# A feature-cross network on one core: a fifth PSUM bank for layer 2, products that read SBUF, and a sum split between GpSimd and VectorE

## The reference

```
x0 = e                                   # (512, 39, 16)
z  = einsum('bfd,bgd->bfgd', x0, xk)     # every pair of fields, kept per embedding column d
x1 = einsum('bpd,pm->bmd', z(x0, x0), f0)
x2 = einsum('bpd,pm->bmd', z(x0, x1), f1)
x3 = einsum('bpd,pm->bmd', z(x0, x2), f2)
h  = concat(sum_d x1, sum_d x2, sum_d x3, dense_ctx)
y  = relu(relu(h @ W1 + b1) @ W2 + b2) @ W3
```

## Time and profile before

| | us |
|---|---|
| median of three runs | 735.24 |
| profiled execution | 735.52 |
| its span, first to last instruction | 733.7 |
| TensorE busy in it | 671.3 (91%) |
| VectorE busy | 626.0 (85%) |
| GpSimd busy | 459.2 (63%) |
| ScalarE busy | 390.5 (53%) |

### The profile page before, as it was taken

The page is one execution under the profiler, slowest core; times in us unless marked ns, Lnnn a source line. Parts: engine busy times, 40 slices in busy tenths (PEclk is TensorE's granted clock), DMA queues, the critical chain, the costliest instruction groups (busy, mean ns, idle before and its releaser), DMA issues.

```text
span 733.7 us, 11667 instructions
## 1 busy us (share of the span) xinstructions
PE 671.3 (91%) x3072; PEld 523.1 (71%) x3072; DVE 626.0 (85%) x2018; ACT 390.5 (53%) x1163; POOL 459.2 (63%) x404
## 2 busy tenths in 40 slices
PE   0187989999999999999999999999999999999977
PEld 0165767676767778787867778787867778787856
DVE  3646999999999898999789898999789898999750
ACT  0325565665656565656456565656456565655321
POOL 6345979586868776775658776775658675552220
PEclk9998999999999999999999999999999999999989
DMA  9814640404040313112030312112040303000000
GB/s 145 155 37 123 208 107 8 106 6 105 7 106 7 97 17 78 34 47 66 5 105 7 99 14 77 35 42 70 5 106 5 104 10 88 16 1 0 1 1 0
DMA packets 70261, 41.27 MB, mean 56 GB/s; under 512 B 47298, under 2 KB 55042, under 8 KB 70067
## 3 DMA queue, kind: packets, MB, share of 16 engines
q1 hardware_dynamic: 60438, 36.45, 19.7%
q0 software_dynamic: 5248, 1.29, 2.1%
q10 hardware_dynamic: 4508, 2.80, 2.0%
HBM read 38.55 MB, written 1.94 MB: 55 GB/s over the span
## 4 chain that ended last, share of the span: by engine, by line
PE 67%; DVE 19%; issue 5%; DMA 3%; POOL 2%; ACT 2%; ACTq 1%; SPq 0%; DVEq 0%; POOLq 0%
PE y L779 17%; PE y L781 14%; PE y L780 14%; DVE scaled L682 14%; PE late L797 4%; PE side L786 3%; PE acc L754 3%; PE acc L753 3%; PE acc L759 3%; PE side L743 2%; DMA s_sb<-in_w_dram 2%; PE late L808 2%; DVE z L652 1%; PE late L830 1%; DVE x_parts L658 1%
## 5 line engine op out<-in xcount | busy, mean ns | idle before, releaser
L682 DVE SCALAR_TENSOR_TENSOR scaled<-y,x_rows,scaled 128x128 f32<-128x128 f32 x1728 | 465.4, 342 | 53.5 <-PE y L781 35.6
L526 ACT ACTIVATE scaled<-y,x_rows 128x128 f32<-128x128 f32 x768 | 218.8, 367 | 165.0 <-PE y L781 150.3
L779 PE MATMUL y<-w_hi,x_parts 128*128 128x512 f32 (+1 forms) x640 | 277.7, 434 | 18.2 <-DVE scaled L682 8.8
L781 PE MATMUL y<-w_hi,x_parts 128*128 128x512 f32 (+1 forms) x640 | 249.0, 389 | 0.0
L780 PE MATMUL y<-w_lo,x_parts 128*128 128x512 f32 (+1 forms) x640 | 248.6, 389 | 0.0
L426 POOL TENSOR_TENSOR z_parts<-z,z_parts 117x512 fp32r<-117x512 f32 (+1 forms) x108 | 139.5, 1291 | 88.8 <-ACT z_parts L480 67.1
L779 PEld LDWEIGHTS y<-w_hi,x_parts 128*128 128x128 f32 x640 | 120.8, 189 | 80.8 <-DVE scaled L682 50.6
L415 POOL DMA_INDIRECT emb_quads<-in_small_tables_dram,quad_rows x144 | 138.0, 959 | 32.7 <-issue 15.5
L781 PEld LDWEIGHTS y<-w_hi,x_parts 128*128 128x128 f32 x640 | 120.7, 189 | 24.9
L434 POOL TENSOR_TENSOR sum<-scaled 128x512 f32<-128x512 f32 x64 | 82.8, 1293 | 84.0 <-DVE scaled L682 83.6
L780 PEld LDWEIGHTS y<-w_lo,x_parts 128*128 128x128 f32 x640 | 121.5, 190 | 14.2
(11 more groups left out here) (42 smaller groups left out, 352.0 us busy)
## 6 DMA issues: line engine op xcount, KB each, us to landing
z<-x_turned SPq DMA_DIRECT2D x309, 78.0 KB
x_three<-x_turned SPq DMA_DIRECT2D x48, 78.0 KB
x_turned<-emb_quads SPq DMA_DIRECT2D x160, 8.0 KB
w_sb<-in_w_dram SPq DMA_DIRECT2D x1, 2496.0 KB, 9.6
emb_quads<-in_small_tables_dram,quad_rows POOLq DMA_INDIRECT x144, 2.4
x_turned<-emb_singles SPq DMA_DIRECT2D x96, 2.0 KB
s_sb<-in_w_dram ACTq DMA_DIRECT2D x9, 160.0 KB, 8.4
z<-x_turned ACTq DMA_DIRECT2D x11, 78.0 KB
```

Of the source, the lines that this page charges most:

```text
L526: done = act.activation(scaled[:, k % 2, BY_ACT.index(j), i * M:(i + 1) * M], y2[n % RING][:, i * M:(i + 1) * M], ACT.Copy, scale=x0_rows[ ...
L682: dve.scalar_tensor_tensor(part, y2[n % RING][:, i * M:(i + 1) * M], x0_f, part, ALU.mult, ALU.add).then_inc(terms_in, 1)
L779: pe.matmul(dst, x1_hi[:, t % 2, cols], hi, start=True, stop=False)
L781: pe.matmul(dst, x1_lo[:, t % 2, cols], hi, start=False, stop=True).then_inc(y_ready, 1)
```

## The change

The bank of `three_ps` goes to the ring, which has five banks. ScalarE's 16 copies into it are gone; the products read `x0_three` in SBUF, so both their inputs lie in SBUF, and the semaphore `three_up` is replaced by the arrival of the DMA (for VectorE) and the count of products (for SyncE, which reuses the buffer). After `fold_three` GpSimd adds the two halves of `sum4` into `sum2` (256 columns), and VectorE adds the two 128-column halves of that in place of the reduction, one slot later (slot 5). The last block's three additions are all VectorE's.

```diff
-RING = 4
+RING = 5
-X2_AT = 4
+X2_AT = 5
...
+        sum2 = sb("sum2", [P, 2 * M])
...
-        three_ps = ps("three_ps", [P, COLS])
...
             def three(u):
                 if u >= 2:
-                    sp.wait_ge(three_up, u - 1)
+                    sp.wait_ge(prod, C0 * (u - 1))
...
                 pool.tensor_tensor(sum4[:, :], sum4[:, :], scaled[:, k % 2, 2, :], ALU.add).then_inc(four_in, 1)
+                pool.wait_ge(four_in, 2 * k + 2)
+                pool.tensor_tensor(sum2[:, :], sum4[:, 0:2 * M], sum4[:, 2 * M:4 * M], ALU.add).then_inc(two_in, 1)
...
-            fold_three(BLOCKS - 1)
...
-            def three(u):
-                act.wait_ge(three_in[u % 2], 48 * (u // 2 + 1))
-                if u > 0:
-                    act.wait_ge(prod, C0 * u)
-                copy(three_ps[0:3 * F, :], x0_three[0:3 * F, u % 2, :]).then_inc(three_up, 1)
...
                 if c == 0:
-                    dve.wait_ge(three_up, u + 1)
+                    dve.wait_ge(three_in[u % 2], 48 * (u // 2 + 1))
                 dve.wait_ge(a_in[c], rounds(c, u))
                 k = depth(c)
-                dve.tensor_tensor(z[0:k, c, :], z[0:k, c, :], three_ps[0:k, :], ALU.mult).then_inc(prod, 1)
+                dve.tensor_tensor(z[0:k, c, :], z[0:k, c, :], x0_three[0:k, u % 2, :], ALU.mult).then_inc(prod, 1)
...
-                dve.wait_ge(four_in, 2 * k + 2)
+                dve.wait_ge(two_in, k + 1)
                 if k >= 2:
                     dve.wait_ge(s_ready, k - 1)
-                dve.tensor_reduce(x2_sb[:, k % 2, :], sum4[:, :].rearrange("p (f m) -> p m f", f=FPB),
-                                  AX_X, ALU.add).then_inc(x2_in, 1)
+                dve.tensor_tensor(x2_sb[:, k % 2, :], sum2[:, 0:M], sum2[:, M:2 * M], ALU.add).then_inc(x2_in, 1)
...
+            def last_x2(k):
+                dve.wait_ge(terms_in, dve_terms(BANKS * k + BANKS - 1))
+                dve.wait_ge(four_in, 2 * k + 1)
+                dve.tensor_tensor(sum4[:, :], sum4[:, :], scaled[:, k % 2, 2, :], ALU.add).then_inc(four_in, 1)
+                dve.wait_ge(four_in, 2 * k + 2)
+                dve.tensor_tensor(sum2[:, :], sum4[:, 0:2 * M], sum4[:, 2 * M:4 * M], ALU.add).then_inc(two_in, 1)
+                x2_of(k)
...
-            x2_of(BLOCKS - 1)
+            last_x2(BLOCKS - 1)
```

More of the change, by code:

```diff
@@ L84 @@
 ROWS_AT = 33
-THREE_AT = 38
-FIRST_THREE_AT = 2
 DIAG_AT = (1, 2, 4, 5, 7, 8, 10, 11)
@@ L282, in cross_network @@
         three_in = [sem(f"three_in_{i}") for i in range(2)]
-        three_up = sem("three_up")
         a_in = [sem(f"a_in_{i}") for i in range(C0)]
@@ L298, in cross_network @@
         four_in = sem("four_in")
+        two_in = sem("two_in")
         x2_in = sem("x2_in")
@@ L576, in _ @@
                 turned_rows(act, 0, c)
-            three(0)
             for c in range(C0):
@@ L605, in _ @@
                         spread_rows(t, DIAG_AT.index(s))
[L606 to L609, removed]
                     if g > 0:
```

## The result

The changed kernel takes 770.57 us, the median of four runs (767.50 to 772.73), against 735.06 (733.14 to 735.31) for the kernel before on the same chip: a ratio of 1.0486, interval 1.0444 to 1.0527, or 35.5 us more. The forecast was 719, with a range up to 740.

A forecast was written before the change was run, and what follows sets the result against it. VectorE was taken to decide at the turn between tiles, TensorE for the rest of a tile. The terms, 22.2 − 3.0 − 5.2 + 1.3 + 1.0 = 16.3 us off the profiled 735.52, gave 719 us, range 702 to 740.

The forecast's parts named there:

- products from SBUF (with the holds of x2): VectorE's two-SBUF products and short additions wait 2.9 us a tile for GpSimd, mostly hidden; 0.2 us a tile, 3.0 us lost.
- fifth bank: At the turn between tiles TensorE runs one bank further before waiting for VectorE: 0.69 us a tile gained, over 15 tiles.
- short sum on VectorE: x2 by a 0.29 us addition, not a 1.073 us reduction: 0.79 us a tile gained at the turn between tiles.
- GpSimd late at the contraction: GpSimd's added work makes low parts reach TensorE's contraction 1.3 us late in four tiles of 16: 5.2 us lost.
- the new tail: At the kernel's end, three VectorE additions replace GpSimd's fold and the reduction: 1.4 us against 2.39, 1.0 us less.
- the one sum at the turn: Of four block sums a tile, only that between tiles, where VectorE decides, shortens the chain: 0.79 us a tile.
- the choice between the ends: Extra bank's gain at the turn between tiles: from 0 to one bank of VectorE's work, 1.13 us; 0.69 taken.
- cover: VectorE's 2.0 us of idle time behind the product stretch was to hide 0.5 us of extra work a tile.
- VectorE's waits win: Rival: products and short additions each wait about half a GpSimd addition, 6.0 us a tile; 751 us, chance 0.18.
- No wait in the other direction: Rival: GpSimd never holds VectorE, which gets 3.15 us a tile for nothing; 700 us, chance 0.17.
- GpSimd sets the pace: Rival: GpSimd is 1.3 us late at the contractions in every tile, 20 us lost; 734 us, chance 0.15.
- Once only: Start and end of the kernel: first product 1.3 us earlier without ScalarE's copy, final sum 1.0 us shorter.

The follow-up runs named there:

- the run of the slot alone: Kernel before with x2's reduction at slot 5 in place of 4, nothing else: 746.71 us, ratio 1.0151.
- the third experiment: Kernel before with products reading x0 from SBUF and a ring of five banks, reduction of x2 still at slot 4: 744.66 us, ratio 1.0120.
- the first experiment: Kernel before with only the products reading x0 from SBUF, four banks and the reduction at slot 4 kept: 753.14 us, ratio 1.0249.
- the lead given back: Changed kernel with `s_block` one slot later too (19 slots behind the block's start, not 18), x2 still at slot 5: 758.78 us, ratio 1.0340.
- the second experiment: Kernel before with the sum split, VectorE's short addition at slot 5 and the three final VectorE additions; products from PSUM, four banks: 725.79 us, ratio 0.9855.

## Why the prediction was wrong, step by step

The parts, taken one after the other along the runs above, against what the prediction gave them:

| step | forecast us | measured us | from |
|---|---|---|---|
| products from SBUF (with the holds of x2) | +3.0 | +17.4 to 18.1, products alone | 735.1 to 735.8, to 753.1 |
| fifth bank | −10.4 (15 × 0.69) | −8.5 | 753.1 to 744.7 |
| short sum on VectorE | −11.8 (15 × 0.79) | −9.3 beside held products, −12.3 alone | 744.7 to 735.3; 735.1 to 722.8 |
| x2 one slot later | 0, named as an end of the bank's gain | +35.2 | 735.3 to 770.6 |
| GpSimd late at the contraction | +5.2 | 4.2 waited in all | view of waits |

The runs of the table's first four lines lead from the kernel before to the changed one, so their differences add up to the loss.

**The short sum was right in size.** 12.3 us alone against 11.8; the 12.3 holds the new tail too, forecast at 1.0 by itself, and an x2 of 0.447 us in place of 0.29, so the closeness is in part luck. The cause given for it, that only the one sum at the turn pays, is not shown apart.

**The fifth bank was about right at slot 4 and had little to win at slot 5.** The sentence that failed is the choice between the ends: "0, if the step that needs x2 stops TensorE first (x2 now comes a bank later)". That end was the true one, and it went below nothing: the bank of VectorE's work that was put ahead of x2 is a cost of its own. With x2 at slot 5 even a ring of four leaves 13.1 us of waits for the banks, by the run of the slot alone; no run takes the fifth bank out of the changed kernel. The profile before could have shown the cost. TensorE waited 5.3 us in all at `s_block`, and the prediction gave that place no price of its own; but a wait that is rare says nothing of how much room there is before it becomes common. One block before, x2 on VectorE's timeline and `s_block` on TensorE's:

```profile
387.89 1.08 DVE L690 TENSOR_REDUCE x_sb<-sum 128x128 f32<-128x512 f32 x1
```

```profile
389.04 0.31 PEld L786 LDWEIGHTS side<-diag,x_sb 128*128 128x128 f32 x2
```

x2 ends at 388.97, 0.07 us ahead of its reader. In 60 of the 64 blocks this room is under 1.13 us (four multiply-adds), in 30 under 0.34. An estimate from these: an x2 that comes 1.13 us later and is 0.79 shorter, as forecast, ends 0.34 later and makes TensorE stop in about half the blocks; held to its 1.18 us it ends some 1.24 later, more room than all but four blocks have. The forecast of the waits for the banks, "down from 50.6 to about 28", is near the 29.8 of the third experiment, whose kernel is another one, and was overshot by the change (15.2) for the wrong reason: TensorE stopped somewhere else first.

**The waits of the two-SBUF instructions were mis-sized and their cover was not there.** Products: 112 × (1.027 − 0.677) = 39.2 us. x2, against its free 0.28: 64 × (0.885 − 0.28) = 38.7 us. Together 78 us, 4.9 a tile, where 2.9 was taken from estimates of 1.7 and 4.1. Two reasons. The estimate let every instruction meet a random or an as-before point of GpSimd's additions, with half an addition left; x2 at slot 5 instead starts inside a low part of GpSimd's in 40 of 64 blocks (411.80 and 411.90 above), and mostly pays nearly a whole one, because both follow the same product by about the same time: the low part behind ScalarE's copy of it and a gather (done at 411.61 and 411.78), x2 behind the bank of four multiply-adds that comes next (410.86 to 411.97). And some products waited for more than one addition (last section). The cover failed too: the "2.0 us of idle time" that was to hide 0.5 us a tile hid less than a third of the first experiment's 1.6 us a tile, and in the changed kernel's tiles it did not shrink at all. That a late product delays the banks behind it at once, while the idle lies elsewhere in the tile, is a reading of the timelines and was not tried by itself.

**The two costs nearly add up.** Of the 35.2 us of the later slot, x2's holds are 19.0 (the run with the reduction of 256 columns). The other 16.2 lie between that run and the one at slot 4. They hold the slot itself, which cost 11.5 us where nothing was held and 11.8 by the lead given back, and an estimate of up to 3.8 for the reduction being longer than the addition at slot 4 (64 × (0.414 − 0.355)). VectorE's account in the three profiled executions agrees: from slot 4 to the reduction at slot 5 its busy time grows from 629.5 to 635.6 us and its idle time from 106.8 to 114.1; with the held addition in place of the reduction the busy time grows to 656.2 and the idle time stays, 113.4. So the holds appear as VectorE's work and the slot mostly as its waiting. Whether each also makes the other worse, no run shows.

**The rivals.** "VectorE's waits win" had the mechanism and the amount: it asked for 4.8 us a tile to decide and got 4.9, and its VectorE work of 40.5 us a tile is 39.9 to 40.7 in three of four. Its time, 751, fell short since it allowed VectorE 0.5 us of idle a tile where 2.3 to 2.4 came; 2.1 to 2.25 had been there before. "No wait in the other direction" is refuted by the first experiment. "GpSimd sets the pace", which asked for 20 us, is refuted by the 4.2 us of waits, although GpSimd got slower as feared (short addition 0.823 us, gathers 1.079 from 0.959).

**Once only.** The first product started at 65.00 against 65.19, not the 1.3 us earlier that was forecast: its own chunk of rows was the late one, 4.65 us of waiting. At the end VectorE's three additions and TensorE's start:

```profile
741.42 0.69 DVE L684 TENSOR_TENSOR sum<-sum,scaled 128x512 f32<-128x512 f32 x1
742.15 0.42 DVE L686 TENSOR_TENSOR sum<-sum 128x256 f32<-128x256 f32 x1
742.60 0.29 DVE L678 TENSOR_TENSOR x_sb<-sum 128x128 f32<-128x128 f32 x1
```

0.69, 0.42 and 0.29 us, as forecast to the hundredth; with the gaps 1.47 us against 2.39 in the earlier trace rows. GpSimd is idle there, so these are also the free durations of the forms that are held elsewhere.

## What to carry to other kernels

Before an operand is moved from PSUM to SBUF, see whether the VectorE instruction then has two SBUF inputs and what GpSimd starts beside it; put it down as held for whole GpSimd additions, above all where both are released by the same event, or use a form with one SBUF input (here a reduction of 256 columns, 0.41 us and never held). A longer ring pays up to the next thing that its filler needs from the same reader: move that producer later and the ring's gain is gone, or move its consumer along with it. Of a change in several parts, time each alone: one of these three was worth 1.5% by itself, and 2.5% with its reader moved along.

## What the hardware showed unexpectedly

Three products, four tiles apart, took 3.63 us (at 124.20, 293.89 and 467.59, each on the chain that ended last). The first of them on VectorE's timeline, and GpSimd's beside it, in the changed kernel:

```profile
124.20 3.63 DVE L640 TENSOR_TENSOR z<-z,x_three 117x512 f32<-117x512 f32 x1
```

```profile
123.75 0.96 POOL L413 DMA_INDIRECT emb_quads<-in_small_tables_dram,quad_rows  x1 [0.16 <-POOL sum L432]
124.72 1.30 POOL L424 TENSOR_TENSOR z_parts<-z,z_parts 117x512 fp32r<-117x512 f32 x1
125.97 1.29 POOL L439 TENSOR_TENSOR sum<-sum,scaled 128x512 f32<-128x512 f32 x1
127.35 1.07 POOL L441 TENSOR_TENSOR sum<-sum 128x256 f32<-128x256 f32 x1
```

The product began 0.52 us before the first addition, and yet both full additions passed it, back to back. It ended at 127.83, after the gap of 0.09 us ahead of the short addition, which in turn was stretched from 0.74 to 1.07. By contrast the product at 415.22 of the changed kernel took its free 0.68 us inside a gather (414.80 to 415.75) behind which no addition was ready until 417.10. In the second experiment x2, begun at 392.38 inside a gather with a low part starting at 392.53, took 1.60 us. But a gather ahead is not enough. In the first experiment a product began 0.17 us before a `fold_two` that stood behind a gather, and it was the addition that was stretched; 12 more such products there, 0.17 to 0.32 us ahead, kept their 0.67 to 0.69 us too:

```profile
118.91 0.67 DVE L639 TENSOR_TENSOR z<-z,x_three 117x512 f32<-117x512 f32 x1
```

```profile
118.10 0.96 POOL L413 DMA_INDIRECT emb_quads<-in_small_tables_dram,quad_rows  x1
119.08 1.66 POOL L432 TENSOR_TENSOR sum<-scaled 128x512 f32<-128x512 f32 x1
```

The traces of the seven runs whose products read SBUF give an order, taken by the addition that follows the gather without a gap. Ahead of a `fold_two` products were held when they began up to 0.14 us before it and ran free from 0.17 us on; ahead of a `fold_three` held up to 0.40 and free from 0.44; ahead of a low part held up to 0.53 us, and no case lies between that and a product's own 0.68. So an addition that stands behind a gather counts as first against a product that begins shortly before it, and how shortly differs by the addition. Where GpSimd had been idle before a `fold_three` and not in a gather, products 0.16 to 0.17 us ahead of it ran free, all 14 in the changed kernel. Why, no run shows. Additions without a gap between them did not let VectorE in.

Gathers are held as well: 51 of 144 take more than 1.1 us, each of them beside a VectorE instruction with two SBUF inputs, where 3 did before; their mean is 1.079 us in place of 0.959.
